# Pair weights in 64 KB pieces behind the gathers, and three groups of products ahead of five chunks' transposes, in a one-core recommender tower

## The reference, cut to what matters

```python
e = jnp.stack([tbl_f[ids[:, f]] for f in range(32)], axis=1)     # 512 x 32 x 64, f32
p, q = e[:, rows, :], e[:, cols, :]                              # the 496 pairs i < j
pij = jnp.einsum('bpe,dpe,bpd->bp', p, kernel, q)                # one 64 x 64 matrix a pair
z = pij @ W.T + b                                                # 496 -> 256
h = jnp.concatenate([z, dense_ctx], axis=1)
h = jnp.maximum(h @ W_top1 + b_top1, 0.0)                        # 272 -> 512
h = jnp.maximum(h @ W_top2 + b_top2, 0.0)                        # 512 -> 256
y = h @ W_top3                                                   # 256 -> 1
```

## Time and profile before

| what | value |
|---|---|
| median of 3 runs | 269.88 us (267.64 to 270.34) |
| the profiled execution's own time | 268.16 us |
| its span, first to last instruction | 266.3 us |
| PE busy | 245.6 us, 92% |
| DVE busy | 171.2 us, 64% |
| POOL busy | 142.0 us, 53% |
| ACT busy | 43.6 us, 16% |
| mean granted TensorE clock | 0.968 of 2.4 GHz |
| from HBM | 15.75 MB, 59 GB/s over the span |

### The profile page before, as it was taken

The page is one execution under the profiler, slowest core; times in us unless marked ns, Lnnn a source line. Parts: engine busy times, 40 slices in busy tenths (PEclk is TensorE's granted clock), DMA queues, the critical chain, the costliest instruction groups (busy, mean ns, idle before and its releaser), DMA issues.

```text
span 266.3 us, 3316 instructions
## 1 busy us (share of the span) xinstructions
PE 245.6 (92%) x1262; PEld 89.1 (33%) x1262; DVE 171.2 (64%) x173; ACT 43.6 (16%) x74; POOL 142.0 (53%) x213
## 2 busy tenths in 40 slices
PE   3999899986769999949999999999999999999996
PEld 1234233322133333312332333333333323333474
DVE  2887746762616687843676878868888858880120
ACT  3686830301010102001010020010100100000121
POOL 4798877768897858376894497888100000000000
PEclk9999999998959999995999999999999999999999
DMA  6541152643131162806019300110000000000000
GB/s 169 173 118 43 25 130 64 161 112 97 22 91 29 28 170 76 197 15 177 20 30 248 76 20 23 24 20 22 10 0 2 0 0 0 4 0 0 2 0 0
DMA packets 9626, 15.97 MB, mean 60 GB/s; under 512 B 3890, under 2 KB 4534, under 8 KB 9610
## 3 DMA queue, kind: packets, MB, share of 16 engines
q1 hardware_dynamic: 6116, 12.32, 17.8%
q0 software_dynamic: 3328, 3.41, 6.0%
q10 hardware_dynamic: 166, 0.02, 0.1%
HBM read 15.75 MB, written 0.00 MB: 59 GB/s over the span
## 4 chain that ended last, share of the span: by engine, by line
PE 54%; DMA 21%; POOL 20%; issue 4%; ACT 0%
PE t_ps L320 27%; DMA gathered<-in_tbl,ids_sb 20%; PE sum_ps L341 15%; POOL gathered L258 14%; POOL rest_sb L265 6%; PE t_ps L380 3%; PE tp_ps L303 2%; PE tp_ps L348 1%; PE t_ps L389 1%; PE t_ps L348 1%; PE t_ps L328 1%; PE t_ps L324 1%; DMA ids_sb<-in_ids 1%; PE tp_ps L389 1%; PE sum_ps L389 1%
## 5 line engine op out<-in xcount | busy, mean ns | idle before, releaser
L507 DVE TENSOR_TENSOR prod<-t_ps,x_sb 128x1024 f32<-128x1024 f32 x120 | 139.9, 1217 | 54.1 <-PE t_ps L321 45.5
L258 POOL DMA_INDIRECT gathered<-in_tbl,ids_sb x104 | 100.0, 961 | 45.1 <-DMA gathered<-in_tbl,ids_sb 28.8
L320 PE MATMUL t_ps<-x_sb,k_sb 64*128 64x512 f32 x240 | 119.6, 632 | 0.8 <-issue 0.4
L321 PE MATMUL t_ps<-x_sb,k_sb 64*128 64x512 f32 x240 | 119.7, 633 | 0.0
L320 PEld LDWEIGHTS t_ps<-x_sb,k_sb 64*128 64x128 f32 x240 | 43.2, 194 | 67.1 <-issue 41.8
L341 PE MATMUL sum_ps<-prod,sel_sb 128*32 128x512 f32 x496 | 60.3, 604 | 0.0
L321 PEld LDWEIGHTS t_ps<-x_sb,k_sb 64*128 64x128 f32 x240 | 43.1, 194 | 0.0
L265 POOL MEMSET rest_sb<- 128x320 f32 x104 | 41.9, 402 | 0.1
L450 ACT COPY x_sb<-tp_ps 128x512 f32<-128x512 f32 x15 | 8.8, 586 | 127.0 <-PE tp_ps L303 75.4
L341 PEld LDWEIGHTS sum_ps<-prod,sel_sb 128*32 128x32 f32 x496 | 13.0, 110 | 43.7 <-issue 24.8
L494 DVE TENSOR_SCALAR k_sb<-ids_bc,iota_sb 125x512 f32<-125x512 f32 x42 | 22.6, 579 | 5.6 <-PE tp_ps L291 2.1
(11 more groups left out here) (47 smaller groups left out, 73.1 us busy)
## 6 DMA issues: line engine op xcount, KB each, us to landing
k_sb<-in_kern SPq DMA_DIRECT2D x32, 256.0 KB, 4.0
gathered<-in_tbl,ids_sb POOLq DMA_INDIRECT x104
w_sb<-in_w SPq DMA_DIRECT2D x2, 512.0 KB
k_sb<-in_tbl SPq DMA_DIRECT2D x3, 280.0 KB
k_sb<-in_tbl SPq DMA_DIRECT2D x3, 224.0 KB
w_pairs_sb<-in_w_pairs SPq DMA_DIRECT2D x1, 512.0 KB
ctx_sb<-in_ctx_rows SPq DMA_DIRECT2D x1, 192.0 KB
w_ctx_sb<-in_w_ctx_rows SPq DMA_DIRECT2D x1, 192.0 KB
```

Source lines behind the costliest of these rows:

```text
L258: pool.indirect_dma_start(gathered[:, n % G_RING, t, f * EMB:(f + 1) * EMB], None, tables[field], bass.IndirectOffsetOnAxis(ap=ids_sb[:, t ...
L320: pe.matmul(t[:, 0, :], k_sb[low, k, :], x_sb[low, a, :], start=True, stop=True)
L321: pe.matmul(t[:, 1, :], k_sb[high, k, :], x_sb[high, a, :], start=True, stop=True).then_inc(t_ready, 1)
L507: dve.tensor_tensor(prod[:, g % PROD_RING], t_ps[:, g % T_RING], q, ALU.mult).then_inc(prod_ready, 1)
```

## The change

Two things change, and some waits with them.

**Weights.** Slices 0 and 1 are as they were. Slices 2 to 15 come in 112 pieces of 64 KB (64 rows of 1 KB), eight to a slice. Piece p waits for the landing of gather 8 + p x 88 // 112, so about five pieces are issued for four gathers, and some gathers release two. `filled` is waited for only once, before slice 8 (where the one-hot data shares the memory). All the late loads follow the last gather. PE waits for all eight pieces of a slice at its first use.

**Order.** For chunks 6 to 10 the fill stands three groups behind the chunk's first group instead of two or three ahead. The list of steps now has ("sums", g) as a step of its own, so that a fill can stand between a group and its sums. PE waits at a chunk's first group only for the copies of the chunks before it.

```diff
-FIRST_CHUNK = [min(GROUP[g][0] for g in range(GROUPS) if BLOCK_OF[g] >= s * KS) for s in range(SLICES)]
-K_EARLY = 4
+AHEAD = range(6, 11)
-LATE_LARGE = 3
+PIECES = 8
+PIECES_FROM, GATHERS_AHEAD = 2, 8
+GATHERS = 2 * BT * (CHUNKS - ONE_HOTS)
...
+def fill_at(c):
+
+
+    return FIRST_GROUP[c] + T_RING if c in AHEAD else FIRST_GROUP[c] - min(LEAD, (c - 1) // 2)
...
-        while chunks < CHUNKS and (chunks < max(2, ONE_HOTS) or g >= FIRST_GROUP[chunks] - min(LEAD, (chunks - 1) // 2)):
+        while chunks < CHUNKS and (chunks < max(2, ONE_HOTS) or g >= fill_at(chunks)):
             steps.append(("fill", chunks))
             chunks += 1
         steps.append(("group", g))
+        if chunks in AHEAD and g + 1 == fill_at(chunks):
+            steps.append(("fill", chunks))
+            chunks += 1
+        steps.append(("sums", g))
...
+            pieces = [(s, q, half) for s in range(PIECES_FROM, SLICES) for q in range(PIECES // 2) for half in range(2)]
+            width = 2 * KS // PIECES
+            for p, (s, q, half) in enumerate(pieces):
+                k = GATHERS_AHEAD + p * (GATHERS - 2 * GATHERS_AHEAD) // len(pieces)
+                sp.wait_ge(rows_in[k % ROWS_RING], 16 * (k // ROWS_RING + 1))
+                if s == SLICES // 2 and q == half == 0:
+                    sp.wait_ge(filled, ONE_HOTS)
+                n = ((2 * s + half) * KS + q * width) * P
+                at = KS * s + q * width
+                sp.dma_start(k_sb[half * EMB:(half + 1) * EMB, at:at + width, :].rearrange("p g m -> p (g m)"),
+                             kern[:, n:n + width * P]).then_inc(k_in[s], 16)
+            for r in range(ROWS_RING):
+                sp.wait_ge(rows_in[r], 16 * (GATHERS // ROWS_RING))
+            for dst, src in LATE:
+                sp.dma_start(dst, src).then_inc(late_in, 16)
...
-                        pe.wait_ge(k_in[s], 32)
+                        pe.wait_ge(k_in[s], 16 * (2 if s < PIECES_FROM else PIECES))
...
                 if g == FIRST_GROUP[c]:
+                    pe.wait_ge(x_ready, 2 * c)
+                if within:
                     pe.wait_ge(x_ready, 2 * (c + 1))
```

More of the change, by code:

```diff
@@ L224, in _ @@
             sp.dma_start(sel_sb[:], selector).then_inc(sel_in, 16)
-            for s in range(SLICES):
+            for s in range(PIECES_FROM):
                 if s == 1:
                     sp.wait_ge(filled, 1)
[L228 to L231, removed]
                 for half in range(2):
@@ L235, in _ @@
                                  kern[:, n:n + KS * P]).then_inc(k_in[s], 16)
-                late = s - (SLICES - LATE_LARGE - 1)
-                for dst, src in LATE[late:late + 1 if late < LATE_LARGE else None] if late >= 0 else ():
-                    sp.dma_start(dst, src).then_inc(late_in, 16)
+            pieces = [(s, q, half) for s in range(PIECES_FROM, SLICES) for q in range(PIECES // 2) for half in range(2)]
[13 more added lines that the diff above has]
+                sp.dma_start(dst, src).then_inc(late_in, 16)
             sp.wait_ge(y_kept, 1)
@@ L358, in _ @@
                         turn(n)
+                elif kind == "group":
+                    products(n)
                 else:
-                    products(n)
                     for q in reduced_after(n) if n not in WITHIN else ():
@@ L454, in _ @@
                     act.copy(own_sb[rows, n % SET // 2, :], from_ps[rows, :]).then_inc(x_ready, 1)
-                else:
+                elif kind == "sums":
                     for q in reduced_after(n):
```

## The result

The changed kernel takes 259.95 us (median of 4 runs, 257.76 to 260.73) against 270.11 us for the kernel before, measured beside it. The ratio is 0.9633, with a 95% interval of 0.9581 to 0.9685: 3.7% faster. The profiled execution took 259.84 us, with a span of 258.0. The forecast was 263.6 us, with a range of 259.2 to 267.8.

A forecast was written before the change was run, and what follows sets the result against it. The prediction took the kernel to be bound by gathers early and PE late. It summed 268.16 - 11.8 - 7.1 + 10.6 - 0.3 + 3.4 = 263.0 us, plus 0.6 carried: 263.6 us, range 259.2 to 267.8.

The forecast's parts named there:

- The waits for gathers go: PE's three waits at the fills of chunks 6, 7 and 10 vanish, -11.8 us, with their clock losses, -7.1 us.
- The gathers' pace: From gather 15 on, gathers start every 1.50 to 1.55 us instead of 1.79; gather 71 starts near 115 us.
- The holes: PE waits for DVE's product behind the late fills of chunks 6 to 10, mostly 2.2 us each, +10.6 us together.
- The extra 0.5 us at chunk 6: Three groups follow before any sums and DVE is slower than PE: 2 x 0.23 us more, a hole of 2.7 us.
- The clock: TensorE's clock falls in two of the four large holes at the smallest price seen, 2 x 1.7 = +3.4 us.
- The weaker wait: At a chunk's first group PE waits only for earlier chunks' copies: -0.3 us, range 0 to 0.7.
- The 0.6 us carried over from the median: The median stood 1.7 us above the profiled execution; a third of that, 0.6 us, was added to the forecast.
- By itself that would remove most of the three waits: Fills of chunks 6 to 10 asked for some 7 to 8 us later would alone remove most waits for gathers.
- 249.3 us "at best": With pieces alone the gathers are ahead and no holes arise: 268.16 - 18.9 = 249.3 us at best.
- slow gathers: Rival: pieces meet every gather, pace stays 1.79, PE waits 4.3 us at chunk 11's fill; 267.4 us, chance 0.11.
- A low clock throughout: Rival: each of PE's holes brings a clock fall at the highest price, 2.9 us; 274.7 us, chance 0.05.
- No fall at all: Rival: PE's holes, shorter than the old waits, cost no clock; 260.2 us, chance 0.22.

The follow-up runs named there:

- the order alone: The changed kernel with the weights and late loads of the kernel before, so late fills and weaker wait only: 265.7 us, 0.9889 of the kernel before.
- the kernel with no late fill: The changed kernel with no chunk's fill behind its first groups, so pieces and weaker wait only: 255.89 us, 0.9527 of the kernel before.
- the pieces alone: The kernel before with the weights' part of the change alone, order and waits for copies as before: 256.45 us, 0.9574 of the kernel before.
- eight late fills: The changed kernel with the fills of chunks 12, 13 and 14 also three groups behind the first group: 269.92 us, 1.0046 of the kernel before.
- the fastest kernel: The changed kernel with the fills of chunks 6 to 10 one group behind the chunk's first group: 250.33 us, 0.9353 of the kernel before.

## Why the prediction was right

In terms of the profiled execution the sum was 263.0 us, and 259.84 came. The mechanism was right: the pieces free the gathers, and the late fills put shorter holes in the place of the waits. The size was off by 3.2 us, and the measured 259.95 us lies near the lower end of the range, beside the 260.2 of a rival that the profile rules out.

- *The waits for gathers go.* Right: 11.8 us and the three low stretches behind them are gone.
- *The gathers' pace.* Right: 1.54 us, forecast 1.50 to 1.55. Gather 71 starts at 118.04 instead of 115: 1.1 us of that it had at gather 15 (31.77 instead of 30.7), and 1.9 comes from the one wait at 107.57, whose cause is open. A gather beside a piece was put at 2.6 to 2.8 us. The median landing of all gathers is 2.5, the longest 4.8. The Trainium skill's 0.95 us for 64 KB ("DMA: Bandwidth & Descriptors", section Bandwidth), added in full to each gather, made a pace of 1.67. The trace doesn't bear that out here: gathers start every 1.50 us while pieces land too (18 steps of 1.50 from 53.11 to 80.02). The advice of the Trainium skill there, batches of a megabyte, is given for the share of the peak bandwidth. In this kernel, which waits for single gathers, pieces of 64 KB beat those of 256 KB by 3.7 us.
- *The holes.* Right in place and cause, somewhat too long: 2.03 us instead of 2.2, and 9.1 instead of 10.6 in all. DVE starts 0.14 us behind the copy, as forecast (63.71 + 0.58 to 64.43), and PE goes on after 2.69 instead of 2.8 us. The extra 0.5 us at chunk 6, where DVE would be slower than PE, hardly shows. The second group behind the fill starts at 66.84, some 0.2 us late, and there the clock falls, so that a group takes 1.6 us or more against DVE's 1.14.
- *The clock.* Two stretches were forecast at 1.7 us each. From 65.71 to 70.34 three groups took 4.63 us, and from 87.02 to 89.79 they took 2.77, which makes 1.9. The sums at 93.54 lasted to 96.75 instead of 1.85 us, and the row behind them 0.3 more, which makes 1.7. That is 3.5 instead of 3.4. The size of one fall came from rows. Their number did not: two was taken because 2.2 us lay between what had brought a fall and what had not, and that it came out is luck in part. The same five holes brought three low stretches in the run of the order alone, and one execution of the changed kernel (257.76 us) has a mean granted clock of 0.993 instead of 0.986 or 0.987, as kernels with one low stretch have.
- *The weaker wait* was mis-sized: "removes 0.3 us ... its range is 0 to 0.7". PE reached the fill of chunk 5 at 47.49 instead of 49.65, and of these 2.16 us 0.56 lie before its first group (34.98 instead of 35.54). So 1.6 us are the wait's, at the first groups of chunks 2, 3 and 4. A single idle row stood for all of them. But by itself it moves nothing, as its own run shows: it counts only once PE is late for nothing else.
- *The rest*: the start, 0.56 us earlier, is no effect of the change: in the kernel with no late fill, which has the same code up to there, PE comes to the fill of chunk 3 at 37.62 us, and in the changed one at 36.90. The end from chunk 11 on came as forecast, 128.7 us. The differences, 1.5 + 1.3 + 0.56 less 0.1 for the clock, make up the 3.2 us that were missing. The 0.6 us carried over from the median were not there: the median is 0.1 us above the profiled execution. SP's 0.6 us for one transfer was too much for the pieces (0.465), which changes nothing.

The forecast's side remarks fared less well. "By itself that would remove most of the three waits", on the order: of the three, 1.6 us at chunk 7 is left in the run of the order alone. But new waits of 2.45 us at chunk 5 and 1.83 at chunk 11, whose fills stand early as before, leave 5.9 of 11.8 us in all. And 249.3 us "at best" for the pieces alone was 256.45: the gathers at full pace still keep the fill of chunk 7 waiting for 4.1 us. The direction, pieces alone faster than the whole, is that of the medians, and the kernel with no late fill bears it out.

The rivals: slow gathers needed a pace of 1.79 and a wait at chunk 11, and neither came. A low clock throughout would have shown five stretches, and there were two. No fall at all (260.2 forecast) would have been near the time, but the profile has two falls; what made it that short were the shorter holes, the weaker wait and the earlier start.

## What to carry to other kernels

When a small latency-bound stream feeds an engine, send the bulk transfers in pieces that fit in the small stream's slack, each released by its progress: that alone, with the late loads moved back, was worth 12 us here. Work moved in front of a late input must not take the last buffer. With three buffers one group in front cost nothing, two about 1.1 us and three 2.0 us at each place, because the way from the input through copy and product needs cover. Two edits aimed at the same wait don't add up; after the first has removed it, ask of the second what it still costs.

## What the runs showed that was not expected

Waits of PE of only 2 us, with work all the time before and after, brought half of TensorE's clock, but not every time. Here are two, of which the longer brought no fall (the granted clock is the third number from the end). First the order alone, PE's wait of 2.45 us at the fill of chunk 5 and the stretch behind it:

```profile
48.98 0.63 PE L314 MATMUL tp_ps<-ident_sb,gathered 128*128 128x128 f32 x4 [2.45 <-DMA gathered<-in_tbl,ids_sb]
48.98:52.50 3.52, 3.52 (x26) 1.16 (x26) 1.23 (x1) 1.17 (x2) 3.19 (x5) 1.00 0.45 129
```

Then the kernel with no late fill, a stretch behind the fill at 59.29 us, for which PE waited 2.02:

```profile
60.20:64.00 3.80, 3.80 (x12) 1.56 (x10) 2.31 (x2) 0.81 (x2) 3.47 (x6) 0.56 0.27 70
```

In the profiles of all twelve kernels, in the part with the groups, PE waited 20 times for 2.0 to 2.5 us, and a low stretch came with 12 of these. One came with each of the 12 waits of 2.9 us or more, and none with those of 1.9 us or less, except where a longer wait stood right behind. In the changed kernel it was two of five holes, with eight late fills four of eight, in the order alone three of five. What decides between 2.0 and 2.5 us these traces don't show. So a hole's price here is 1.4 times its length in the changed kernel (9.1 us of holes and 3.5 of clock), and up to 1.7 times with eight late fills. With the waits at 0.5 us or less the profile of the fastest kernel has a clock of 1.0 throughout; one of its other executions has 0.993.
